# Softplus of a state-space layer: six of eight correction subtractions on GpSimd instead of VectorE, and "one plus the exponential" on VectorE in every round

## Chip, cores and metric

The kernel runs on one core of one Trainium2 chip. The metric is the device time of one execution in microseconds (us); the number given for a kernel is the median of several runs. Five engines matter: TensorE (PE in the profile's rows, PEld for its weight loads), VectorE (DVE), ScalarE (ACT), GpSimd (POOL) and SyncE (SP), which only issues transfers.

## What is computed

A small language-model tower on 8 x 256 tokens, 192 channels wide: embedding and position code, one Mamba layer that scans in both directions, and a mixture of eight experts. The part that the change touches is the step size `dt` of the scan, one array for each direction:

```python
proj = u @ x_proj_w
dt = jax.nn.softplus(proj[..., :DT_RANK] @ dt_w + dt_b)
...
y = selective_scan(u, dt, A, Bm, Cm)       # dA = exp(dt * A); h = dA * h + dt * u * B
```

`u` has 384 inner channels, kept as 3 blocks of 128 partitions.

## The kernel before

The tokens are cut into four groups of 512 (`NG = 4`, `GT = 512`), and each group has two directions, so the softplus stage has eight rounds, n = 0 to 7, with group n // 2 and direction n % 2. One round works on an array of 128 partitions x 1536 float32 (three blocks of 512 tokens). [...]

- TensorE: three products into PSUM (L1543). They wait on `s_pl`, which says that VectorE has read round n-2 out of the same banks.
- ScalarE: |x| block by block (L1232), e = exp(-|x|) (L1234, into `sp_e`, signalled by `s_e`), then log(1 + e) (L1240, into `dt`, signalled by `s_l`).
- w = 1 + e. In rounds 0, 2, 4, 6 and 7 VectorE computes it (L797); in rounds 1, 3 and 5 (`BY_ACT`) ScalarE does (L1242, signalled by `s_w`).
- The correction (w - 1) - e, which is what rounding lost in 1 + e: L798 on VectorE, signalled by `s_c`. This is the function `correction`.
- `add_pos` (L807): dt = max(x, 0) + log(1 + e), read from PSUM and `dt`, on VectorE, signalled by `s_pl`.
- `subtract_correction` (L814): dt = dt - correction, on VectorE, signalled by `s_dt`. In rounds 4 and 5 a product dt * u of rounds 0 and 1 follows (`times_u`, L817).

`sp_e` and `sp_w` have three buffers each (`SP = 3`), so ScalarE waits on `s_dt` of round n-3 before it begins round n.

The order on each engine is the order in which its program is written; the engines meet only at semaphores. GpSimd gathers the embedding rows first (L561), then helps with one mix of the embedding (L583, L586), adds the residual (L597), and has nothing in the softplus stage. It comes back in the scan, where it multiplies each scanned state by C (L625).

The scan follows (L851 on VectorE). Its first item waits for round 7 on VectorE (`s_dt` of 8), for ScalarE's decays exp(dt * A) (L1278, which wait for `s_dt` of 7) and for the products of TensorE (L1451 and L1573 in `x_blocks_of`). The first two `x_blocks_of` wait on `s_pl` of 7 and 8, since they write into banks that `add_pos` reads. ScalarE then evacuates transposes of dt * u (L1211), and goes on to the second unit of the scan (L1261, L1264, L1278).

Of the kernel before, what the change touches and what calls it, by code (L numbers as in the profile page):

```python
# [8 lines left out]
ALU = mybir.AluOpType  # L9
ACT = mybir.ActivationFunctionType  # L10
# [28 lines left out]
SP = 3  # L39
# [36 lines left out]
def build(nc, tok, emb, spos, pos, chan, w_in, gb_in, xproj, dt_w, gb_out, w_out, merge, w_route, emb_t,  # L76
          energy, fatigue, gates12, b1, b2, wf1, ws1, hf1, wf2, ws2, hf2, gates_dram, b_rows, x_rows, y_rows, out):
    ctx = ExitStack()
    with ctx:
# [3 lines left out]
        def sem(name):  # L83
            return ctx.enter_context(nc.semaphore(name))
# [62 lines left out]
        def cut(shape, dt=FP32, parts=P):  # L147
            n = 1
            for s in shape:
                n *= s  # L150
            words = n if dt != BF16 else n // 2
            assert used[0] + words <= ARENA, used[0]
            v = arena[0:parts, used[0]:used[0] + words]
            used[0] += words
            if dt != FP32:
                v = v.bitcast(dt)
            if len(shape) == 2:
                v = v.rearrange("p (a b) -> p a b", b=shape[1])
            if len(shape) == 3:
                v = v.rearrange("p (a b c) -> p a b c", b=shape[1], c=shape[2])  # L160
            if len(shape) == 4:
                v = v.rearrange("p (a b c d) -> p a b c d", b=shape[1], c=shape[2], d=shape[3])
            return v
# [6 lines left out]
        dt_all = [[cut([DB, GT]) for _ in range(2)] for _ in range(NG)]  # L170
# [47 lines left out]
        sp_e, sp_w = zip(*[[cut([DB, GT]) for _ in range(2)] for _ in range(SP)])  # L218
# [114 lines left out]
        s_e = sem("softplus_exp_ready")  # L333
        s_c = sem("softplus_corr_ready")
        s_pl = sem("softplus_pos_and_log_added")
        s_w = sem("softplus_one_plus_exp_ready")
        s_l = sem("softplus_log_ready")
        s_lb_ps = sem("dt_and_b_product")
        s_lb = sem("dt_and_b_rows_ready")
# [5 lines left out]
        s_dt = sem("dt_ready")  # L345
# [73 lines left out]
        s_passed = sem("waits_passed")  # L419
        FRONT_LOADS, PAR_LOADS = 2, 34  # L420
        DT_BANK = 2
        BY_ACT = (1, 3, 5)
        FIRST_BANKS = (0, 0, 0, 1, 0, 1, 0, 1)

        c_rows = b_rows
# [130 lines left out]
        def _(pool):  # L556
            g_ = nc.gpsimd
            st = Steps(pool, p_step)
# [35 lines left out]
            for h in range(2):  # L594
                half = slice(HT * h, HT * (h + 1))
                pool.wait_ge(s_lnin, h + 1)
                g_.tensor_tensor(resid[:, half, :], resid[:, half, :], ln_in[:, half, :], ALU.add).then_inc(s_res, 1)  # L597

            def times_u(g, d):

                pool.wait_ge(s_dtu_ps, TG * (2 * g + d))
                g_.tensor_tensor(dtu, dt_all[g][d], u_all[g], ALU.mult).then_inc(s_dtu, 1)
# [5 lines left out]
            for i in range(ITEMS):  # L608
# [7 lines left out]
                e, part = divmod(i - 3 * DB, EACH * DB)  # L616
# [42 lines left out]
        def _(dve):  # L659
            v = nc.vector  # L660
            st = Steps(dve, v_step)
# [128 lines left out]
            def correction(n):  # L790

                w, e = sp_w[n % SP], sp_e[n % SP]
                dve.wait_ge(s_e, n + 1)
                if n in BY_ACT:
                    dve.wait_ge(s_w, BY_ACT.index(n) + 1)
                else:
                    st.then(v.tensor_scalar(w, e, 1.0, None, ALU.add))  # L797
                v.scalar_tensor_tensor(w, w, -1.0, e, ALU.add, ALU.subtract).then_inc(s_c, 1)  # L798

            def add_pos(n):  # L800

                g, d = divmod(n, 2)
                dt = dt_all[g][d]
                dve.wait_ge(s_l, n + 1)
                bank = ps[:, DT_BANK + DB * d:DT_BANK + DB * (d + 1), :].rearrange("p a b -> p (a b)")
                flat = dt.rearrange("p a b -> p (a b)")
                v.scalar_tensor_tensor(flat, bank, 0.0, flat, ALU.max, ALU.add).then_inc(s_pl, 1)  # L807

            def subtract_correction(n):
                g, d = divmod(n, 2)  # L810
                dt = dt_all[g][d]
                dve.wait_ge(s_pl, n + 1)
                dve.wait_ge(s_c, n + 1)
                v.tensor_tensor(dt, dt, sp_w[n % SP], ALU.subtract).then_inc(s_dt, 1)  # L814

            def times_u(d):
                v.tensor_tensor(dtu_b if d else dtu, dt_all[0][d], u_all[0], ALU.mult).then_inc(s_dtu, 1)  # L817

            for n in range(2 * NG):
                if n in BY_ACT:  # L820
                    add_pos(n)
                    correction(n)
                else:
                    correction(n)
                if n == 0:
                    dve.wait_ge(s_rset, 1)
                    st.then(v.tensor_copy(gain_1[:], ps[:, 1, 0:E]))
                    v.tensor_copy(w_route_sb[:, :, E + DR + 1:RC], ps[0:KC, 1, E:(1 + KT) * E].rearrange("p (k e) -> p k e", k=KT)).then_inc(s_wr, 1)
                if n not in BY_ACT:
                    add_pos(n)  # L830
                subtract_correction(n)
                if n in (4, 5):
                    dve.wait_ge(s_dt, n - 3)
                    times_u(n - 4)
# [266 lines left out]
        def _(act):  # L1101
            a = nc.scalar
            a.preload_act_table_set("natural_log_exp_and_others")
            st = Steps(act, a_step)
# [61 lines left out]
            def keep_lb(g):  # L1166
                act.wait_ge(s_lb_ps, g + 1)
                if g >= 2:

                    act.wait_ge(s_c_st[g % 2], 32)  # L1170
                a.activation(lb[g % 2], ps[:, 0, :], ACT.Identity, scale=row_scale[:], bias=row_one[:]).then_inc(s_lb, 1)
# [36 lines left out]
            def keep_first_dtu_t(i):  # L1208

                act.wait_ge(s_dtu_ps, i + 1)  # L1210
                a.activation(dtu_t[0][i // TG][:, i % TG, :], ps[:, FIRST_BANKS[i], 0:DI], ACT.Copy).then_inc(s_dtu_t, 1)  # L1211

            def keep_bt(g):
                act.wait_ge(s_bt_ps, g + 1)
                a.activation(bt[:, TG * g:TG * (g + 1), :], ps[:, 1, 0:TG * 2 * NS].rearrange("p (t n) -> p t n", t=TG), ACT.Copy).then_inc(s_bt, 1)

            a.preload_act_table_set("natural_log_exp_and_others")
            for g in range(NG):
                for d in range(2):
                    n = 2 * g + d  # L1220
                    if n >= SP:

                        act.wait_ge(s_dt, n - SP + 1)

                    if n == 0:
                        act.wait_ge(s_u, NG * DB)
                    if n == 2:
                        act.wait_ge(s_sz_st, 16 * NG)
                    dt = dt_all[g][d]
                    for blk in range(DB):  # L1230
                        act.wait_ge(s_dt_ps, DB * n + blk + 1)
                        st(a.activation(dt[:, blk, :], ps[:, DT_BANK + DB * d + blk, :], ACT.Abs))  # L1232
                    st.wait()
                    a.activation(sp_e[n % SP], dt, ACT.Exp, scale=-1.0).then_inc(s_e, 1)  # L1234
                    if d == 1:
                        keep_bt(g)
                        if g == NG - 1:
                            keep_first_dtu_t(1)
                    act.wait_ge(s_e, n + 1)
                    a.activation(dt, sp_e[n % SP], ACT.Ln, bias=1.0).then_inc(s_l, 1)  # L1240
                    if n in BY_ACT:
                        a.activation(sp_w[n % SP], sp_e[n % SP], ACT.Identity, bias=1.0).then_inc(s_w, 1)  # L1242
                    if d == 0 and g + 1 < NG:
                        keep_lb(g + 1)
                    elif d == 0:
                        act.wait_ge(s_res, 2)
                        act.wait_ge(s_xn, NG)
                        act.wait_ge(s_xn_ps, NG)
                        keep_first_dtu_t(0)
# [196 lines left out]
        def _(pe):  # L1446
# [111 lines left out]
            def x_blocks_of(i):  # L1558

                u, blk = divmod(i, DB)  # L1560
                g, _, d = unit_of(u)
                cols = slice(P * blk, P * blk + P)
                if blk == 0:
                    pe.wait_ge(s_x_t, u + 1)
                    pe.wait_ge(s_dtu_t, 8 * g + TG * (d + 1))
                if i >= 2:

                    pe.wait_ge(s_scan, i - 1)
                bank = X_BANK + PAIR * (i % 2)
                for t in range(TG):  # L1570
                    transpose(ps[:, bank, P * t:P * t + P], x_t[u % 2][:, t, cols], P)
                for t in range(TG):
                    last = mm(ps[:, bank + 1, P * t:P * t + P], dtu_t[g % 2][d][:, t, cols], b_diag[u % 2][:, t, :], start=True, stop=True)  # L1573
                last.then_inc(s_x_ps, 1)
# [270 lines left out]
```

## Time and profile before

| | us |
|---|---|
| median of 3 runs (lowest, highest) | 904.82 (903.65, 904.99) |
| the profiled execution, device time | 903.25 |
| its span, first to last instruction | 901.5 |
| softplus stage on VectorE, first L797 to first scan L851 | 94.0 to 144.3 |
| busy in that stretch: VectorE, ScalarE, GpSimd | 49.35, 48.75, 0.00 |
| GpSimd from the end of L597 to its first L625 | 66.4 to 146.7 |

The page of the profile gives busy shares over the whole span. This change lies within one stretch of about 50 us, so the shares are to be read from that stretch. A row's duration runs from the start of an instruction on its engine to its end; where it waits inside for something that no semaphore shows, the wait is in the duration.

### The profile page before, as it was taken

To read this page: it belongs to the slowest core of one execution; us is meant where nothing else is said; L and a number is where in the kernel's file an instruction comes from. 1 tells how busy PE (TensorE), PEld (TensorE's weight loads), DVE (VectorE), ACT (ScalarE), POOL (GpSimd) and SP (SyncE) were. 2 spreads that over 40 slices of the span, in tenths; PEclk is the share of its full clock that TensorE was granted. 3 is DMA by queue.
4 is the path that set the end of the run, shared out by engine and by line. 5 is a ranking of instruction groups with operands and counts; after the bars stand their busy time and mean duration, and the time that the engine had idled before them with its cause. 6 is when DMAs were issued, how large, how long until landed. Compare 5 with 4: busy or idle time off the path is not lost.

```text
span 901.5 us, 16654 instructions
## 1 busy us (share of the span) xinstructions
PE 778.9 (86%) x6060; PEld 706.4 (78%) x6061; DVE 730.8 (81%) x871; ACT 648.5 (72%) x1261; POOL 535.1 (59%) x343
## 2 busy tenths in 40 slices
PE   0389777899999999989999899996956999999990
PEld 0133336899998999989999899995855899999990
DVE  3788899789999899988999999998938455555554
ACT  0365999999999999989999999992331444444421
POOL 6430004799988999969999799892000444444420
PEclk9999988999999999999999999997955899999996
DMA  4003103355674754745746466376450111111106
GB/s 87 3 30 111 9 27 123 89 137 175 148 212 149 165 191 123 195 140 130 210 113 163 159 180 187 118 167 230 136 171 9 40 44 44 44 44 44 44 23 218
DMA packets 46453, 104.43 MB, mean 116 GB/s; under 512 B 16448, under 2 KB 25176, under 8 KB 46392
## 3 DMA queue, kind: packets, MB, share of 16 engines
q1 hardware_dynamic: 35784, 74.67, 25.6%
q0 software_dynamic: 8352, 27.07, 15.1%
q10 hardware_dynamic: 2256, 1.87, 0.6%
q8 instruction: 38, 0.62, 0.3%
q14 instruction: 23, 0.19, 0.1%
HBM read 83.77 MB, written 19.82 MB: 115 GB/s over the span
## 4 chain that ended last, share of the span: by engine, by line
PE 47%; DVE 22%; ACT 17%; POOL 7%; issue 4%; DMA 2%; DVEq 0%; ACTq 0%; POOLq 0%; SPq 0%
PE ps L1451 15%; PE ps L1755 8%; PE ps L1573 8%; DVE arena L851 8%; ACT arena L1278 6%; PE ps L1738 6%; POOL arena L625 5%; ACT arena L1261 4%; PE ps L1743 4%; ACT arena L1264 3%; PE ps L1471 2%; PE ps L1474 1%; DVE stats L672 1%; DVE arena L798 1%; PE ps L1673 1%
## 5 line engine op out<-in xcount | busy, mean ns | idle before, releaser
L625 POOL TENSOR_TENSOR arena<-arena 128x1024 f32<-128x1024 f32 x192 | 395.3, 2285 | 117.3 <-DVE arena L851 114.0
L851 DVE TENSOR_TENSOR_SCAN arena<-arena,ps 128x1024 f32<-128x1024 f32 x192 | 426.3, 2277 | 20.1 <-PE ps L1573 16.9
L1451 PE MATMUL ps<-ident,arena 128*128 128x128 f32 (+3 forms) x2622 | 349.3, 280 | 79.2 <-ACT arena L1139 37.7
L1451 PEld LDWEIGHTS ps<-ident,arena 128*128 128x128 f32 (+3 forms) x2622 | 299.7, 144 | 100.6 <-issue 52.0
L1278 ACT ACTIVATE arena<-arena,neg_a 128x510 f32<-128x510 f32 x384 | 241.0, 708 | 0.1
L629 POOL DMA_INDIRECT arena<-x_rows,arena x39 | 37.8, 970 | 160.2 <-DVE arena L1035 79.6
L1573 PE MATMUL ps<-arena,ln_in 128*128 128x128 f32 x768 | 104.0, 279 | 0.0
L1573 PE MATMUL ps<-arena 128*128 128x128 f32 x768 | 101.4, 275 | 0.0
L1573 PEld LDWEIGHTS ps<-arena,ln_in 128*128 128x128 f32 x768 | 96.0, 196 | 0.0
L1573 PEld LDWEIGHTS ps<-arena 128*128 128x128 f32 x768 | 93.3, 192 | 0.0
L1755 PE MATMUL ps<-arena,ln_in 128*128 x468 | 82.7, 327 | 0.8 <-DVE arena L1066 0.8
L1264 ACT ACTIVATE arena<-ident,arena 128x128 f32<-128x128 f32 x256 | 81.0, 388 | 0.0
L1755 PEld LDWEIGHTS ps<-arena,ln_in 128*128 128x128 f32 x468 | 75.1, 190 | 1.2 <-issue 1.1
L1261 ACT ACTIVATE arena<-ln_in,arena 128x384 f32<-128x384 f32 x128 | 68.1, 605 | 3.1 <-PE ps L1573 2.7
L1261 ACT ACTIVATE arena<-arena 128x384 f32<-128x384 f32 x128 | 67.9, 602 | 2.6 <-PE ps L1573 2.5
L637 POOL DMA_INDIRECT y_rows<-arena x39 | 38.5, 988 | 30.9 <-DVE arena L1066 19.1
L1409 ACT ACTIVATE arena<-ps 128x256 f32<-128x256 f32 x39 | 15.0, 384 | 56.2 <-PE ps L1451 56.2
L1053 DVE TENSOR_TENSOR ln_in<-ps,arena 128x384 f32<-128x384 f32 x40 | 22.1, 554 | 40.1 <-PE ps L1743 40.1
L1053 DVE TENSOR_TENSOR ln_in<-ps,ln_in 128x384 f32<-128x384 f32 x38 | 21.0, 553 | 34.3 <-PE ps L1743 34.3
L1417 ACT ACTIVATE arena<-arena 128x1158 f32 x20 | 23.4, 1170 | 33.4 <-issue 14.2
L1061 DVE SCALAR_TENSOR_TENSOR ln_in<-ln_in 128x384 f32<-128x384 f32 x78 | 43.5, 558 | 2.7
L1417 ACT ACTIVATE ln_in<-arena 128x1158 f32 x19 | 22.2, 1170 | 20.9 <-issue 17.4
(218 smaller groups left out, 882.5 us busy)
## 6 DMA issues: line engine op xcount, KB each, us to landing
arena<-b_rows SPq DMA_DIRECT2D x64, 512.0 KB, 4.0
arena<-ws SPq DMA_DIRECT2D x16, 576.0 KB, 6.3
arena<-wf POOLq DMA_DIRECT2D x16, 576.0 KB, 8.2
arena<-hf POOLq DMA_DIRECT2D x16, 576.0 KB, 7.9
summed_first<-arena SPq DMA_DIRECT2D x8, 576.0 KB, 5.4
summed_second<-arena SPq DMA_DIRECT2D x8, 576.0 KB, 7.3
arena<-summed_second SPq DMA_DIRECT2D x8, 576.0 KB, 5.8
gates_dram<-arena SPq DMA_DIRECT2D x4, 768.0 KB, 3.4
```

Of the source, the lines that this page charges most:

```text
L625: g_.tensor_tensor(state[i % STATES], state[i % STATES], c_bc[u % C_BUFS], ALU.mult).then_inc(s_mul, 1)
L851: v.tensor_tensor_scan(o, a, x, 0.0, ALU.mult, ALU.add).then_inc(s_scan, 1)
L1053: added = v.tensor_tensor(hid, ps[:, H_BANKS[half] + i, 0:HH].rearrange("p (a b) -> p a b", b=P), bias[:, 3 * i:3 * (i + 1)].unsqueeze(2). ...
L1061: v.scalar_tensor_tensor(hid, hid, 0.0, hid, ALU.max, ALU.mult).then_inc(s_h[i], 1)
L1261: a.activation(x_t[u % 2][:, t, :], dtu_t[g % 2][d][:, t, :], ACT.Copy, scale=bt[:, TG * g + t, col:col + 1])
L1264: last = a.activation(b_diag[u % 2][:, t, :], ident[:], ACT.Copy, scale=bt[:, TG * g + t, col:col + 1])
L1278: last = a.activation(out_a[:, n, :, lo:hi], src[:, :, lo:hi], ACT.Exp, scale=neg_a[:, blk, d, PAIR * pair + n:PAIR * pair + n + 1])
L1417: a.activation(w1_cur[half], w1_all[:, bass.ds(e * WC, WC)], ACT.Copy).then_inc(s_wc, 1)
L1451: return mm(o, src, ident[at:at + parts, at:at + parts], start=start, stop=True, is_transpose=True, skip_group_check=True)
L1573: last = mm(ps[:, bank + 1, P * t:P * t + P], dtu_t[g % 2][d][:, t, cols], b_diag[u % 2][:, t, :], start=True, stop=True)
L1738: mm(ps[:, H_BANKS[half] + j // 3, P * (j % 3):P * (j % 3) + P], w1_cur[half][:, P * j:P * j + P], slot_x_t[half][:, 0, :], start=j % 3 == ...
L1755: last = mm(ps[:, 3, 0:C], h_t[half][:, j, :], w2_all[:, bass.ds(e * (HB * C) + j * C, C)], start=j == 0, stop=j == HB - 1)
```

## The change

Four edits. ScalarE no longer computes 1 + e in rounds 1, 3 and 5; VectorE does so in all eight rounds, and the order on VectorE is the same in all (1 + e, correction, add). In rounds 0 to 5 (`BY_POOL = 6`) the subtraction of the correction is issued on GpSimd, in order of n, each waiting for `s_pl` and `s_c` of its round; it is placed behind L597, ahead of the scan. In rounds 6 and 7 it stays on VectorE and waits for the earlier ones (`s_dt` of n).

```diff
-        BY_ACT = (1, 3, 5)
+        BY_POOL = 6
...
+            for n in range(BY_POOL):
+                dt = dt_all[n // 2][n % 2]
+                pool.wait_ge(s_pl, n + 1)
+                pool.wait_ge(s_c, n + 1)
+                g_.tensor_tensor(dt, dt, sp_w[n % SP], ALU.subtract).then_inc(s_dt, 1)
...
                 dve.wait_ge(s_e, n + 1)
-                if n in BY_ACT:
-                    dve.wait_ge(s_w, BY_ACT.index(n) + 1)
-                else:
-                    st.then(v.tensor_scalar(w, e, 1.0, None, ALU.add))
+                st.then(v.tensor_scalar(w, e, 1.0, None, ALU.add))
                 v.scalar_tensor_tensor(w, w, -1.0, e, ALU.add, ALU.subtract).then_inc(s_c, 1)
...
                 dve.wait_ge(s_pl, n + 1)
                 dve.wait_ge(s_c, n + 1)
+                dve.wait_ge(s_dt, n)
                 v.tensor_tensor(dt, dt, sp_w[n % SP], ALU.subtract).then_inc(s_dt, 1)
...
             for n in range(2 * NG):
-                if n in BY_ACT:
-                    add_pos(n)
-                    correction(n)
-                else:
-                    correction(n)
+                correction(n)
...
-                if n not in BY_ACT:
-                    add_pos(n)
-                subtract_correction(n)
+                add_pos(n)
+                if n >= BY_POOL:
+                    subtract_correction(n)
                 if n in (4, 5):
                     dve.wait_ge(s_dt, n - 3)
                     times_u(n - 4)
...
                     a.activation(dt, sp_e[n % SP], ACT.Ln, bias=1.0).then_inc(s_l, 1)
-                    if n in BY_ACT:
-                        a.activation(sp_w[n % SP], sp_e[n % SP], ACT.Identity, bias=1.0).then_inc(s_w, 1)
```

VectorE's program before, from the first softplus instruction through round 1 (`arena` is the buffer that holds dt, e and w, `ps` is PSUM; the names in brackets are the semaphores waited for):

```order
L797 TENSOR_SCALAR arena<-arena 128x1536 [waits softplus_exp_ready]
L798 SCALAR_TENSOR_TENSOR arena<-arena 128x1536 [waits vector_step]
L827 COPY gain<-ps 128x8 [waits router_setup_product]
L828 COPY w_route_sb<-ps 96x2x8 [waits vector_step]
L807 SCALAR_TENSOR_TENSOR arena<-ps,arena 128x1536 [waits softplus_log_ready]
L814 TENSOR_TENSOR arena<-arena 128x1536 [waits softplus_corr_ready,softplus_pos_and_log_added]
L807 SCALAR_TENSOR_TENSOR arena<-ps,arena 128x1536 [waits softplus_log_ready]
L798 SCALAR_TENSOR_TENSOR arena<-arena 128x1536 [waits softplus_one_plus_exp_ready,softplus_exp_ready]
L814 TENSOR_TENSOR arena<-arena 128x1536 [waits softplus_corr_ready,softplus_pos_and_log_added]
```

The same place after the change (line numbers shift: L799 is 1 + e, L800 the correction, L809 the addition):

```order
L799 TENSOR_SCALAR arena<-arena 128x1536 [waits softplus_exp_ready]
L800 SCALAR_TENSOR_TENSOR arena<-arena 128x1536 [waits vector_step]
L826 COPY gain<-ps 128x8 [waits router_setup_product]
L827 COPY w_route_sb<-ps 96x2x8 [waits vector_step]
L809 SCALAR_TENSOR_TENSOR arena<-ps,arena 128x1536 [waits softplus_log_ready]
L799 TENSOR_SCALAR arena<-arena 128x1536 [waits softplus_exp_ready]
L800 SCALAR_TENSOR_TENSOR arena<-arena 128x1536 [waits vector_step]
L809 SCALAR_TENSOR_TENSOR arena<-ps,arena 128x1536 [waits softplus_log_ready]
```

The subtraction L814 is gone from both rounds, and right behind each addition that reads PSUM now stands the 1 + e of the next round; in round 1 the addition has moved behind the correction.

GpSimd's program after the change, from the residual addition to the first multiplications of the scan (L596 is what was L597, L630 what was L625):

```order
L596 TENSOR_TENSOR resid<-resid,ln_in 128x1536 [waits ln_in_ready,conv_ready,params_loaded]
L596 TENSOR_TENSOR resid<-resid,ln_in 128x1536 [waits ln_in_ready]
L602 TENSOR_TENSOR arena<-arena 128x1536 [waits softplus_corr_ready,softplus_pos_and_log_added] x6
L630 TENSOR_TENSOR arena<-arena 128x1024 [waits scan_done,c_broadcast_loaded_0]
L630 TENSOR_TENSOR arena<-arena 128x1024 [waits scan_done] x2
```

The six subtractions (L602 there) are new in this place; before the change the multiplications of the scan came next.

## Rows read from the trace of the kernel before

**Rows 1.** The page, busy time of each engine over the span.

```profile
PE 778.9 (86%) x6060; PEld 706.4 (78%) x6061; DVE 730.8 (81%) x871; ACT 648.5 (72%) x1261; POOL 535.1 (59%) x343
```

**Rows 2.** Busy time of each engine in the softplus stage.

```profile
core 0: us, PE busy (x) PEld busy (x) DVE busy (x) ACT busy (x) POOL busy (x), PEclk, DMA share, GB/s
94.00:144.30 50.30, 37.51 (x110) 19.58 (x110) 49.35 (x34) 48.75 (x69) 0.00 (x0) 0.83 0.05 15
```

**Rows 3.** Chain that ended last: start, length in us, engine and line.

```profile
104.24 1.76 DVE arena L814
106.00 0.88 DVE arena L797
106.91 1.76 DVE arena L798
108.67 1.68 DVE arena L807
...
136.35 1.15 DVE arena L814
...
145.19 0.88 ACT ln_in L1211 x2
```

**Rows 4.** Groups of instructions in the softplus stage: busy us, mean ns | idle before.

```profile
L814 DVE TENSOR_TENSOR arena<-arena 128x1536 f32<-128x1536 f32 x8 | 14.1, 1759 | 0.5
L798 DVE SCALAR_TENSOR_TENSOR arena<-arena 128x1536 f32<-128x1536 f32 x8 | 14.0, 1754 | 0.2
L807 DVE SCALAR_TENSOR_TENSOR arena<-ps,arena 128x1536 f32<-128x1536 f32 x8 | 14.0, 1751 | 0.2 <-ACT arena L1240 0.2
...
L797 DVE TENSOR_SCALAR arena<-arena 128x1536 f32<-128x1536 f32 x5 | 4.8, 955 | 6.4 <-ACT arena L1234 6.4
...
L1242 ACT ACTIVATE arena<-arena 128x1536 f32<-128x1536 f32 x3 | 4.4, 1472 | 0.0
```

**Rows 5.** Timeline of VectorE, first addition, later subtractions, end of stage: start, us.

```profile
96.97 1.75 DVE L807 SCALAR_TENSOR_TENSOR arena<-ps,arena 128x1536 f32<-128x1536 f32 x1
...
136.35 1.76 DVE L814 TENSOR_TENSOR arena<-arena 128x1536 f32<-128x1536 f32 x1
...
140.69 1.75 DVE L807 SCALAR_TENSOR_TENSOR arena<-ps,arena 128x1536 f32<-128x1536 f32 x1
142.47 1.76 DVE L814 TENSOR_TENSOR arena<-arena 128x1536 f32<-128x1536 f32 x1
144.27 6.64 DVE L851 TENSOR_TENSOR_SCAN arena<-arena,ps 128x1024 f32<-128x1024 f32 x3
```

**Rows 6.** Timeline of VectorE in the embedding, while GpSimd computes too.

```profile
37.81 0.69 DVE L706 TENSOR_TENSOR ln_in<-arena 128x512 f32<-128x512 f32 x1
38.53 1.43 DVE L706 TENSOR_TENSOR arena<-arena 128x512 f32<-128x512 f32 x1
40.00 1.43 DVE L709 TENSOR_TENSOR ln_in<-ln_in,arena 128x512 f32<-128x512 f32 x1
```

**Rows 7.** Timeline of GpSimd in the same stretch.

```profile
37.86 1.56 POOL L583 TENSOR_TENSOR ln_in<-arena 128x512 f32<-128x512 f32 x1 [11.46 <-DVE arena L696]
39.50 1.39 POOL L583 TENSOR_TENSOR arena<-arena 128x512 f32<-128x512 f32 x1
```

**Rows 8.** GpSimd arithmetic of single lines (ns min/median/max), and two of its timeline.

```profile
L602 POOL TENSOR_TENSOR arena<-arena x6: 2907/3226/3564, 178.5 to 451.1; 128x1536 f32<-128x1536 f32 x6
L597 POOL TENSOR_TENSOR resid<-resid,ln_in x2: 3445/3446/3447, 59.5 to 62.9; 128x1536 f32<-128x1536 f32 x2
...
174.61 4.62 POOL L625 TENSOR_TENSOR arena<-arena 128x1024 f32<-128x1024 f32 x2
178.53 3.56 POOL L602 TENSOR_TENSOR arena<-arena 128x1536 f32<-128x1536 f32 x1
```

**Rows 9.** Timeline of ScalarE: exponential of round 1, and the evacuation behind round 7.

```profile
97.66 1.49 ACT L1234 ACTIVATE arena<-arena 128x1536 f32<-128x1536 f32 x1
...
145.19 0.87 ACT L1211 ACTIVATE ln_in<-ps 128x384 f32<-128x384 f32 x2 [0.66 <-PE ps L1451]
```

More of the change, by code:

```diff
@@ L335, in build @@
         s_pl = sem("softplus_pos_and_log_added")
-        s_w = sem("softplus_one_plus_exp_ready")
         s_l = sem("softplus_log_ready")
```

## Prediction

> **What bounds the kernel now.** I read the page first: TensorE is busy 86% of the span, VectorE 81%, ScalarE 72%, GpSimd 59% [rows 1]. None of these says what the change is worth, because it lies within one stretch. So the second view is the busy time between the first L797 and the first scan. There VectorE works 49.35 of 50.3 us, ScalarE 48.75, GpSimd nothing [rows 2]. Third, the chain that ended last: from the addition of round 1 on it runs through VectorE alone (subtract, 1 + e, correction, add, and again), until the subtraction of round 6 at 136.35 hands over to ScalarE and TensorE, which lead to ScalarE's evacuation at 145.19 [rows 3]. VectorE is the bound of the stage, and ScalarE, at 97% of it, is close behind. Whatever happens to VectorE's pace here shifts the whole rest of the kernel; a gain is capped early by ScalarE, a loss is capped by nothing.
>
> **What the edits do on paper.** Durations run start to start, since back-to-back operations on VectorE overlap by some 0.08 us: the chain has L797 from 106.00 to 106.91, and L798 to L807 takes 1.76, L807 to the next 1.68-1.70 [rows 3]. I use 0.95 for 1 + e, 1.70 for the others.
>
> - Six subtractions leave VectorE: 6 x 1.70 = 10.2 us less.
> - Three 1 + e come to VectorE: 3 x 0.95 = 2.9 us more.
> - Three L1242 leave ScalarE: 4.4 us less [rows 4].
> - GpSimd gets six subtractions of 128x1536. Nearest rows: its products of the same shape in the same buffer, 2.907 us at the least, and the residual addition, 3.446 us [rows 8]. The longer ones of L602 are counted from a start that lies inside the operation before: 178.53 is ahead of 174.61 + 4.62 = 179.23, where L625 ends, so that one ran 178.53 + 3.56 - 179.23 = 2.86 us. I take 2.9, because L602 reads and writes the same buffer as the new operation; L597 is the upper end.
>
> If the two engines did not disturb each other, VectorE would have 7.3 us less, ScalarE 4.4 us less, and the stage would gain about 5.
>
> **What they do to each other.** In the embedding both engines work on two-input operations with all operands in SBUF, and they take turns. VectorE's 128x512 operation takes 0.69 us when it is first [rows 6]. The next one starts at 38.53, takes 1.43 and ends at 39.96, while GpSimd's operation of 37.86 ends at 39.42 [rows 6, 7]: it finished 0.54 us behind GpSimd's end, so it stood still until then. GpSimd's next starts at 39.50 and ends at 40.89, which is 0.93 behind VectorE's end at 39.96; VectorE's next starts at 40.00 and ends at 41.43, 0.54 behind 40.89. So one runs while the other stands, for the whole length of an operation, and the one already waiting goes first: GpSimd had asked at 39.50, before VectorE's third operation at 40.00, and was served before it.
>
> In the changed stage the correction (L798) has two SBUF inputs, like those. The addition (L807) reads PSUM and one SBUF input. The scan has that form as well (L851, arena and ps in [rows 5]) and the products of GpSimd under it take their 2.9 us, so I let it run beside GpSimd. For 1 + e (L797) no row shows it beside GpSimd. It has one input, but takes 955 ns where the two-input form takes 1759 for the same 1536 elements [rows 4], so it moves one input at nearly twice the pace, as with both read paths; I take it as excluded too. Below that stands the case that it runs freely (priced under the rivals).
>
> The Trainium skill ("SBUF — State Buffer", section "Who interferes with whom") states that a `tensor_scalar` in a two-port mode takes the port pair that VectorE and GpSimd share, and that the second to issue blocks fully. By that rule the total is the one forecast here; with the exclusion for two-input operations alone it would be that of the third rival. The trace has no row that decides it.
>
> **The sum.** The subtraction of round n may start when the addition of round n has ended. At that moment VectorE goes on with 1 + e of round n+1, and GpSimd asks some 0.1 us later. Whichever gets in first, the correction of round n+1 is behind both: 0.95 + 2.9 + 1.7, and only then comes the addition, 1.7. A round takes 7.2 us, less 0.1 to 0.15 that an operation saves when it was already issued and waited (0.54 against 0.69 above), so 7.1, where it was 0.95 + 3 x 1.7 = 6.05 in the rounds with 1 + e on VectorE and 5.1 to 5.2 in the others. GpSimd's work is on VectorE's path in full. Nothing of it hides under the addition, because the addition of the same round is what it waits for, and the one of the next round is behind a correction that GpSimd has shut out.
>
> Step by step, from the addition of round 0, which ends at 96.97 + 1.75 = 98.72 as before [rows 5]:
>
> - Round 1: e is ready at 97.66 + 1.49 = 99.15 [rows 9], GpSimd holds until 101.75, 1 + e until 102.55, correction 104.25, addition 105.9.
> - Rounds 2, 3, 4: 7.1 each: 113.0, 120.1, 127.2.
> - Round 5: dt * u of round 0 is ahead (1.7): 136.0.
> - Round 6: dt * u of round 1 (1.7), GpSimd (2.85), 1 + e (0.8), correction, addition: 144.8; the subtraction on VectorE ends at 146.5. Its new wait for `s_dt` of 6 costs nothing: GpSimd finished round 5 at 140.5.
> - Round 7: no more GpSimd, 0.95 + 1.7 + 1.8 + 1.75 = 6.2: 152.7, against 142.47 + 1.76 = 144.23 [rows 5].
>
> That is 8.5 us later. The same as a sum: six times 2.9 on (17.4), 10.2 off, 2.9 on, 0.9 off for the six starts that were already issued, and 0.7 off for the small gaps before L814 and L807 (0.5 and 0.2 idle) [rows 4], which go.
>
> **Who waits for that.** ScalarE kept up with rounds of 5.6 us on average, so it keeps up with 7.1, and the 4.4 us it saves are worth nothing. The addition of round 7 ends at 150.9 instead of 140.69 + 1.75 = 142.44, and behind it stand TensorE's second `x_blocks_of` and the transposes that ScalarE takes at 145.19, after waiting 0.66 us for them [rows 9]; that was on the chain, and it moves by the same 8.5. ScalarE's decays wait for the subtraction of round 6, which moves from 136.35 + 1.76 = 138.1 to 146.5 [rows 5], and take less than 4 us, so they are done before the transposes come. On SyncE the loads of C and of the weights behind `s_dt` of 8 shift along. Against the profiled execution, 903.25 + 8.5 = 911.8; the median of the runs lies 1.6 higher, 904.8, so the forecast for a median is 913.3.
>
> With 3.45 for GpSimd's operation it is 6 x 0.55 = 3.3 more, 916.6. The Trainium skill ("GPSIMD Engine Reference", section "Elementwise — side-by-side cycle accounting") has 4497 ns for a two-input add of 2048 elements; as an estimate from that page 1536 take 3.37, and the total would be 916.1. The row of L602 is shorter, that of L597 a little longer than it.
>
> **Rivals.**
>
> 1. *No disturbance that matters* (8%), ending on the other side. The stage gains what ScalarE allows, between its 4.4 us and VectorE's 7.3; about 5, so 899.8. For it: GpSimd is empty here, and in the scan the two engines run together freely. Against: rows 6 and 7. It would decide if the correction, a three-operand form, used the read paths otherwise than L706 does; a round would have to be below 5.6 us.
> 2. *VectorE keeps its turn* (7%): the correction gets in ahead of the waiting GpSimd. Then GpSimd's 2.9 lies over the addition, a round is 0.95 + 1.7 + 2.9 = 5.6, about the average of before, and the total is 904 to 906. Against: the order of service at 39.96.
> 3. *1 + e runs beside GpSimd* (10%): six times 0.8 to 0.95 are hidden, about 5.4: 907.9.
> 4. *The forecast's mechanism with GpSimd near 3.45 us* (13%): 916.6.
>
> The forecast itself has 60%, other outcomes 2%. That leaves slower by over 0.2% (above 906.6; about what this measurement can tell from no change) at 0.86, within 0.2% at 0.05, faster at 0.09. The range runs from 906.5, which takes in rival 3, to 918, which takes in rival 4 with a little for slower handovers.
>
> **What would show it.** The profile after should have GpSimd's six subtractions end about 2.9 us behind the end of VectorE's 1 + e; corrections in rounds 1 to 5 of about 4.5 us instead of 1.75 (or, if GpSimd is served first, 1 + e of about 3.8); additions unchanged at 1.75 and 7.1 us apart; the first scan near 152.7; no idle time of VectorE before 1 + e put down to ScalarE beyond 1 us. Wrong it would be if corrections stay at 1.75 (rival 1), if GpSimd's operations are stretched to 4.6 while rounds stay at 5.6 (rival 2), or if ScalarE or TensorE turn out to be waited for in these rounds.

## The result, and the profile after

The changed kernel takes 914.62 us (median of 4 runs, 914.13 to 915.65), the kernel before 904.24 (4 runs, 903.40 to 904.99): a ratio of 1.0117, with a 95% interval of 1.0099 to 1.0134. On paper the change takes 7 us of work off the engine that bounds the stage, and the kernel gets 10.4 us slower. A second measurement, on another chip (r_after below, 5 runs against 17 of the kernel before), gives 8.5 us and 1.0100, so the size is known to about 2 us only. One of the five runs of a further experiment, d_warm, took 1384 us at a mean granted clock of 0.565; its ratio leaves that run out.

The profiled execution after took 915.65 us, the longest of its four. Its softplus stage begins 1.6 us later than before (first 1 + e at 95.61 instead of 94.02); that lies ahead of everything that was changed, and the last section comes back to it. So times in the stage are compared from its first 1 + e.

The timeline of VectorE after the change (start, length in us, line and operation; L799 is 1 + e, L800 the correction, L809 the addition, L820 dt * u, L850 the scan):

```profile
98.56 1.74 DVE L809 SCALAR_TENSOR_TENSOR arena<-ps,arena 128x1536 f32<-128x1536 f32 x1
100.77 3.34 DVE L799 TENSOR_SCALAR arena<-arena 128x1536 f32<-128x1536 f32 x1 [0.46 <-ACT arena L1233]
104.14 1.76 DVE L800 SCALAR_TENSOR_TENSOR arena<-arena 128x1536 f32<-128x1536 f32 x1
105.82 1.75 DVE L809 SCALAR_TENSOR_TENSOR arena<-ps,arena 128x1536 f32<-128x1536 f32 x1
107.49 0.95 DVE L799 TENSOR_SCALAR arena<-arena 128x1536 f32<-128x1536 f32 x1
108.47 4.34 DVE L800 SCALAR_TENSOR_TENSOR arena<-arena 128x1536 f32<-128x1536 f32 x1
112.74 1.74 DVE L809 SCALAR_TENSOR_TENSOR arena<-ps,arena 128x1536 f32<-128x1536 f32 x1
...
121.98 3.21 DVE L799 TENSOR_SCALAR arena<-arena 128x1536 f32<-128x1536 f32 x1 [0.59 <-ACT arena L1233]
...
128.57 1.75 DVE L820 TENSOR_TENSOR arena<-arena 128x1536 f32<-128x1536 f32 x1
130.24 3.67 DVE L799 TENSOR_SCALAR arena<-arena 128x1536 f32<-128x1536 f32 x1
...
154.34 2.29 DVE L850 TENSOR_TENSOR_SCAN arena<-arena,ps 128x1024 f32<-128x1024 f32 x1 [0.35 <-PE ps L1570]
```

And that of GpSimd, the first two and the fifth of its six subtractions:

```profile
100.39 2.91 POOL L602 TENSOR_TENSOR arena<-arena 128x1536 f32<-128x1536 f32 x1 [32.81 <-DVE arena L809]
107.65 3.55 POOL L602 TENSOR_TENSOR arena<-arena 128x1536 f32<-128x1536 f32 x1 [4.36 <-DVE arena L809]
...
128.74 4.35 POOL L602 TENSOR_TENSOR arena<-arena 128x1536 f32<-128x1536 f32 x1 [4.36 <-DVE arena L809]
```

Read the two together. GpSimd's first subtraction runs from 100.39 to 103.30, undisturbed, in 2.91 us. VectorE's 1 + e was started at 100.77, in the middle of it, and ends at 104.11: 0.81 after GpSimd's end. In the next round VectorE was first: its 1 + e of 107.49 takes its usual 0.95, GpSimd asks at 107.65 and ends at 111.20, which is 2.76 after the end of 1 + e at 108.44. The correction started at 108.47, so behind GpSimd in the queue, and ends at 112.81, 1.61 after GpSimd. The additions, which read PSUM, keep their 1.75. In [rows 4] the same 1 + e took 955 ns on average and the correction 1754.

The chain that ended last, from the products of round 7 to the evacuation of the last transposes:

```profile
137.42 5.50 PE ps L1540 x6
142.92 0.02 issue
142.94 0.61 ACT arena L1231
143.55 0.02 issue
143.57 1.49 ACT arena L1233
...
145.60 1.38 ACT arena L1239
...
151.41 1.09 PE ps L1448 x4
...
157.27 0.88 ACT ln_in L1210 x2
```

Before the change VectorE led until 137.5, and only the last 7.7 us up to this point were ScalarE and TensorE [rows 3]. Now the last 20 us are. The waits in the stage (engine and line, what it waited for, us, times, longest) say why:

```profile
ACT arena L1231 <- PE ps L1540: 14.4, 13, 2.6
PE ps L1540 <- DVE arena L809: 14.2, 5, 3.8
```

TensorE waits 14.2 us for VectorE's additions to free the banks, where it was 7.3 before, and ScalarE waits 14.4 us for TensorE. The last evacuation comes 157.27 - 95.61 = 61.66 us after the first 1 + e, against 145.19 - 94.02 = 51.17: 10.5 later, where the first scan is 58.73 - 50.25 = 8.5 later. In the second profiled execution of the changed kernel (r_after) it is 10.0 and 8.2.

### The profile page after: what moved, and what is told of

Same layout as the page of the kernel before. It is cut to its first block, busy times and chain, and to the rows that moved or that the text cites. A ratio compares the mean times of both kernels' runs of the same rounds, so it can differ in the third digit from the quotient of the medians.

```text
span 913.9 us, 16651 instructions
## 1 busy us (share of the span) xinstructions
PE 782.8 (86%) x6060; PEld 705.7 (77%) x6061; DVE 738.7 (81%) x868; ACT 645.1 (71%) x1258; POOL 556.4 (61%) x349
## 4 chain that ended last, share of the span: by engine, by line
PE 47%; DVE 20%; ACT 20%; POOL 6%; issue 4%; DMA 2%; DVEq 0%; ACTq 0%; POOLq 0%; SPq 0%
PE ps L1448 14%; PE ps L1752 8%; ACT arena L1275 7%; DVE arena L850 7%; PE ps L1570 7%; PE ps L1735 6%; ACT arena L1258 5%; POOL arena L630 4%; PE ps L1740 4%; ACT arena L1261 3%; PE ps L1468 2%; PE ps L1540 1%; PE ps L1471 1%; ACT arena L1283 1%; DVE stats L677 1%
## 5 line engine op out<-in xcount | busy, mean ns | idle before, releaser
L850 DVE TENSOR_TENSOR_SCAN arena<-arena,ps 128x1024 f32<-128x1024 f32 x192 | 426.5, 2276 | 21.8 <-PE ps L1570 16.9
L630 POOL TENSOR_TENSOR arena<-arena 128x1024 f32<-128x1024 f32 x192 | 395.1, 2285 | 54.1 <-DVE arena L850 50.8
L602 POOL TENSOR_TENSOR arena<-arena 128x1536 f32<-128x1536 f32 x6 | 21.6, 3602 | 52.6 <-DVE arena L809 52.6
```

The lines of the kernel that those rows point to most:

```text
L630: g_.tensor_tensor(state[i % STATES], state[i % STATES], c_bc[u % C_BUFS], ALU.mult).then_inc(s_mul, 1)
L850: v.tensor_tensor_scan(o, a, x, 0.0, ALU.mult, ALU.add).then_inc(s_scan, 1)
```

## The experiments

Theory: VectorE and GpSimd take turns, whenever VectorE's operation has two inputs in SBUF or is the 1 + e, and GpSimd reads from SBUF; the loss is GpSimd's reading, laid across VectorE's line. Rivals: the loss comes from dt being ready later; from three VectorE operations in every round; from TensorE and ScalarE feeding the stage.

All runs in one table. "Scan" is the start of the first scan, "evacuation" the start of ScalarE's last evacuation of transposes behind round 7, both from the profiled execution and in us after the first 1 + e. The ratio is to runs of the kernel before on the same chip.

| kernel | scan | evacuation | median us | ratio (95%) |
|---|---|---|---|---|
| before | 50.25 | 51.17 | 904.24 | |
| changed | 58.73 | 61.66 | 914.62 | 1.0117 (1.0099-1.0134) |
| r_after, the same again | 58.40 | 61.19 | 913.79 | 1.0100 (1.0085-1.0114) |
| a_ones_only | 53.07 | 55.36 | 907.2 | 1.0025 (1.0015-1.0036) |
| b_pool_only | 52.37 | 52.70 | 906.51 | 1.0013 (1.0003-1.0022) |
| c_pool_late | 50.64 | 52.59 | 905.52 | 1.0000 (0.9991-1.0009) |
| d_warm | 58.08 | 59.48 | 914.31 | 1.0103 (1.0085-1.0121) |
| r_warm, the same again | 58.06 | 59.79 | 914.46 | 1.0107 (1.0092-1.0123) |
| e_junk_read | 65.52 | 67.24 | 919.82 | 1.0165 (1.0143-1.0188) |
| f_junk_write | 50.26 | 51.61 | 904.53 | 0.9994 (0.9984-1.0004) |
| g_late_act | 48.80 | 49.30 | 903.35 | 0.9984 (0.9976-0.9993) |
| r_late_act, the same again | 48.80 | 49.31 | 903.59 | 0.9978 (0.9969-0.9987) |
| h_late_warm | 50.67 | 51.56 | 904.79 | 0.9996 (0.9985-1.0007) |
| i_late_act3 | 50.22 | 51.44 | 904.39 | 0.9998 (0.9988-1.0008) |

### One half of the change at a time

a_ones_only: 1 + e on VectorE in all rounds, nothing on GpSimd.

```diff
-        BY_POOL = 6
+        BY_POOL = 0
```

> One plus the exponential on VectorE in all eight rounds, all eight subtractions on VectorE, nothing on GpSimd. Taking turns (my theory): without GpSimd nothing is stretched, every 1 + e stays at 0.95 us and every correction at 1.76; VectorE has three more 1 + e (2.9 us) and loses some 0.9 of small gaps, so the first scan is about 2 us later and the time about 906.3. Rival (the loss comes from the chain of three operations in every round and from ScalarE and TensorE feeding it, not from GpSimd): most of the 10 us is here, above 911.

Measured: 1.0025, first scan 2.8 us later (2 were expected; fewer of the small gaps went than the 0.9 us counted, and the scan waits 0.36 us for TensorE), 1 + e and correction at 0.95 and 1.76 throughout. It is a quarter of the loss at most in the time; the rival with most of 10 us here falls.

b_pool_only: the kernel before, with the six subtractions on GpSimd.

```diff
+            for n in range(6):
+                dt = dt_all[n // 2][n % 2]
+                pool.wait_ge(s_pl, n + 1)
+                pool.wait_ge(s_c, n + 1)
+                g_.tensor_tensor(dt, dt, sp_w[n % SP], ALU.subtract).then_inc(s_dt, 1)
...
+                dve.wait_ge(s_dt, n)
...
-                subtract_correction(n)
+                if n >= 6:
+                    subtract_correction(n)
```

> Only the subtractions of rounds 0 to 5 go to GpSimd; ScalarE keeps 1 + e of rounds 1, 3 and 5, and the order in those rounds is add, then correct. Taking turns: in the odd rounds GpSimd's operation lies over the addition that reads PSUM, and in the even ones over nothing, so a pair of rounds takes 0.95 + 2.9 + 1.7 + 1.7 + 2.9 + 1.7 = 11.85 us where it took 11.2; three pairs give about 2 us, time about 906. Rival (GpSimd's operation costs its full length in every round, six times 2.9 less 1.7): 7 us later, 911.

Measured: 1.0013, first scan 2.1 us later, both as expected. The way there was not the expected one. Two of VectorE's rows (L813 is the addition, L803 is 1 + e), and GpSimd's fourth subtraction:

```profile
101.42 1.76 DVE L813 SCALAR_TENSOR_TENSOR arena<-ps,arena 128x1536 f32<-128x1536 f32 x1 [2.00 <-ACT arena L1248]
...
119.96 0.96 DVE L803 TENSOR_SCALAR arena<-arena 128x1536 f32<-128x1536 f32 x1 [3.19 <-ACT arena L1242]
```

```profile
116.91 2.90 POOL L603 TENSOR_TENSOR arena<-arena 128x1536 f32<-128x1536 f32 x1 [1.76 <-DVE arena L804]
```

VectorE waits 7.3 us for ScalarE within this stage, where it was 0.2 before, and GpSimd's first and fourth subtractions lie mostly over such waits. So the expected 2 us came out in part by luck. The same six operations on GpSimd cost 2 us here, and 8.5 - 2.8 = 5.7 on top of a_ones_only in the changed kernel. That shows that the length of GpSimd's operation alone does not set the price. How much of it the additions from PSUM hide, and how much the waits for ScalarE, this run does not separate; the next one moves the operations onto the additions by themselves.

### The same operations, started at another moment

c_pool_late: one number of the changed kernel.

```diff
-                pool.wait_ge(s_c, n + 1)
+                pool.wait_ge(s_c, n + 2)
```

> The changed kernel, but GpSimd's subtraction of round n also waits for the correction of round n+1, so that it starts beside the addition of round n+1, which reads PSUM. Taking turns: a round takes 0.95 + 1.7 + 2.9 = 5.55 us instead of 7.1, corrections stay at 1.76, the 1 + e of the next round is stretched to about 2; the first scan comes about 1 us earlier than in the kernel before, time 903 to 905. Rival (what costs is how long GpSimd takes, or that dt comes late): starting it later can only make it later, 914 or more.

Measured: 1.0000, first scan at 50.64. VectorE's rounds, from its timeline:

```profile
108.44 1.75 DVE L809 SCALAR_TENSOR_TENSOR arena<-ps,arena 128x1536 f32<-128x1536 f32 x1
110.11 2.28 DVE L799 TENSOR_SCALAR arena<-arena 128x1536 f32<-128x1536 f32 x1
112.42 1.76 DVE L800 SCALAR_TENSOR_TENSOR arena<-arena 128x1536 f32<-128x1536 f32 x1
114.10 1.75 DVE L809 SCALAR_TENSOR_TENSOR arena<-ps,arena 128x1536 f32<-128x1536 f32 x1
```

and GpSimd's:

```profile
108.67 2.91 POOL L602 TENSOR_TENSOR arena<-arena 128x1536 f32<-128x1536 f32 x1 [2.75 <-DVE arena L800]
114.33 2.90 POOL L602 TENSOR_TENSOR arena<-arena 128x1536 f32<-128x1536 f32 x1 [2.75 <-DVE arena L800]
```

GpSimd starts with the addition, overlaps all of it, and stretches the next 1 + e by 1.3 us only; additions are 114.10 - 108.44 = 5.66 apart instead of 6.9 to 7.3. GpSimd's operation starts one correction later than in the changed kernel, every dt is ready later against its own round, and the kernel is 9 us faster. That settles between turn-taking and lateness as the cause of the loss. The first scan was expected 1 us earlier than in the kernel before, and comes 0.4 later, since the subtraction of round 6 waits for GpSimd, which the expectation had not counted:

```profile
137.67 1.76 DVE L817 TENSOR_TENSOR arena<-arena 128x1536 f32<-128x1536 f32 x1 [1.51 <-POOL arena L602]
```

Lateness does have a smaller price: ScalarE, which reuses the buffers, waits 0.48 us for GpSimd ahead of round 6 and 1.73 us ahead of round 7, and the evacuation comes 1.4 us later than in the kernel before.

### Reading or being busy

Both add six GpSimd operations to the kernel before, that nothing in the stage waits for; what they write is not used. (SyncE's later weight loads into the same memory also wait for them, but the sixth product ends at 145.42, and those loads wait for the last subtraction, which starts at 159.19.)

```diff
+            for n in range(6):
+                pool.wait_ge(s_pl, n + 1)
+                if n:
+                    pool.wait_ge(s_junk, n)
+                g_.tensor_tensor(scratch, scratch, ones[:].unsqueeze(1).to_broadcast([P, 12, P]), ALU.mult).then_inc(s_junk, 1)
```

In f_junk_write the last line is `g_.memset(scratch, 1.0)`.

> The kernel before, unchanged in what it computes, and beside it six GpSimd products of 128x1536 on memory that nobody uses, each started when the addition of rounds 0 to 5 has ended; nothing waits for them in the stage. Taking turns: 6 x 3.0 = 18 us of reading by GpSimd lie across VectorE's line, less the two additions of rounds 1 and 3 (3.4) and the starts already issued (0.9): the first scan comes about 13.5 us later, time about 918, with VectorE's two-input operations of 4.3 us among them. Rival (the loss comes from dt being ready late, that is from the dependency): nothing, 905.

> The same with a fill of 128x1536 by GpSimd, which reads nothing, in place of the product. If the turns are about reading from SBUF, VectorE's corrections and subtractions keep their 1.76 us, and at most a 1 + e is stretched: below 906.5. If any activity of GpSimd stops VectorE, corrections or subtractions are stretched by the length of the fill.

Measured: e_junk_read 1.0165, first scan 65.52 - 50.25 = 15.3 us later; f_junk_write 0.9994. VectorE in e_junk_read, first around GpSimd's second product, then around its fifth (L823 is the subtraction, L826 dt * u):

```profile
103.85 3.06 DVE L807 SCALAR_TENSOR_TENSOR arena<-arena 128x1536 f32<-128x1536 f32 x1
107.01 4.81 DVE L823 TENSOR_TENSOR arena<-arena 128x1536 f32<-128x1536 f32 x1
...
132.14 1.76 DVE L823 TENSOR_TENSOR arena<-arena 128x1536 f32<-128x1536 f32 x1
133.81 4.98 DVE L826 TENSOR_TENSOR arena<-arena 128x1536 f32<-128x1536 f32 x1
```

GpSimd's fifth product in the same run:

```profile
132.18 5.00 POOL L606 TENSOR_TENSOR arena<-arena,ones 128x1536 f32<-128x1536 f32 x1 [6.04 <-DVE arena L816]
```

It asked 0.04 us after VectorE's subtraction had begun, stood until 133.90, and ran 3.28 us; VectorE's next, started at 133.81, ends 1.61 after it. That is 0.3 us longer than the 3.0 I had used, six times, which is the difference between the 13.5 expected and the 15.3 measured. Nothing depends on these products, so the dependency plays no part.

f_junk_write, GpSimd's first two fills:

```profile
100.41 1.39 POOL L606 MEMSET arena<- 128x1536 f32 x1 [32.77 <-DVE arena L816]
104.17 1.38 POOL L606 MEMSET arena<- 128x1536 f32 x1 [2.38 <-DVE arena L816]
```

and VectorE's subtraction and correction over them:

```profile
100.38 1.76 DVE L823 TENSOR_TENSOR arena<-arena 128x1536 f32<-128x1536 f32 x1
...
104.03 1.75 DVE L807 SCALAR_TENSOR_TENSOR arena<-arena 128x1536 f32<-128x1536 f32 x1
```

Neither is stretched by anything, and the same holds for the other four fills. A GpSimd that is busy with writing alone does not hold VectorE's two-input operations; one that reads does. (A fill is also shorter than the product and does no arithmetic; that difference is not tested apart from the reading.) In this run no 1 + e met a fill, so for that pair it says nothing.

### TensorE's clock

d_warm and r_warm: useless transposes keep TensorE busy ahead of three rounds of the changed kernel.

```diff
+                    if 2 * g + d in (4, 6, 7):
+                        if d:
+                            pe.wait_ge(s_bt, g)
+                        for _ in range(30):
+                            transpose(ps[:, d, 0:P], ident[:], P)
```

> The changed kernel with 30 transposes of the identity, whose results nobody reads, on TensorE ahead of the products of rounds 4, 6 and 7, where it had been idle for 3.5 to 3.8 us and its three products then took 5.17, 4.51 and 5.49 us instead of 2.8. If TensorE's granted clock behind the idle time is what makes the evacuation behind round 7 come 10.5 us later and not 8.5: the products of round 7 take about 2.8 us, round 4 loses its idle 0.6 us on VectorE, and the time is 912 to 913. If it is ScalarE's own work that is late: no change, 914.6.

> The changed kernel once more, on the same chip as the three below, so that each can be set against it. All theories: about 1.2% above the kernel before.

> The kernel with the 30 transposes ahead of rounds 4, 6 and 7 again, beside the changed kernel. TensorE's clock accounts for the 2 us between the first scan (8.5 us later) and the evacuation (10.5): 1.5 to 2 us below the changed kernel. ScalarE's own work accounts for it: equal.

Busy time in one stretch around the products of round 4 (columns: stretch, its length, then busy us and count of PE, PEld, DVE, ACT, POOL, then granted clock), changed kernel:

```profile
110.00:122.00 12.00, 8.20 (x18) 3.65 (x17) 11.37 (x6) 7.16 (x10) 5.28 (x3) 0.72 0.00 0
```

and d_warm:

```profile
110.00:122.00 12.00, 10.22 (x49) 6.26 (x49) 11.93 (x7) 9.08 (x10) 5.28 (x3) 1.00 0.01 1
```

In the changed kernel the mean granted clock of these 12 us is 0.72, a mixture of full speed (2.4 GHz) and half (1.2 GHz), after 3.8 us of idling; with the useless work it is 1.00, and the products of round 4 take 2.84 us instead of 5.17. But the kernel before is not at full speed either, which the expectations left out: in the same 12 us its granted clock is 0.86, its products of round 4 take 4.29 us, and those of round 7:

```profile
126.84 4.54 PE L1543 MATMUL ps<-arena 128*128 128x512 f32 x6 [1.12 <-DVE arena L807]
```

The 0.59 us that VectorE stood idle ahead of round 4 are gone, but r_after, without useless work, does not have them either (its products of round 4 took 4.51 us). The evacuation comes 2.2 us earlier in d_warm than in the changed kernel, and 1.4 us earlier in r_warm than in r_after. In d_warm the products of round 7 still took 4.54 us, against the 2.8 expected. In r_warm they took 2.84, and then TensorE had to wait for VectorE's addition of round 7 (L810 there) before the last products:

```profile
150.68 1.12 PE L1449 MATMUL ps<-ident,arena 128*128 128x128 f32 x4 [1.78 <-DVE arena L810]
```

The time does not follow: 914.46 against 913.79 on the same chip, where 1.5 to 2 us less were expected. In the profiled execution of r_warm 1.8 us come back later, in the scan (last section). So the profiles show that TensorE's clock moves the evacuation by 1.4 to 2.2 us, but that filling the idle time gains anything was not shown, and whether the loss in the scan is chance or a consequence stays open.

> The late version with 30 transposes of the identity on TensorE ahead of the products of rounds 6 and 7. In the late version the evacuation behind round 7 comes 1.4 us later against the start of the stage than in the kernel before, the first scan only 0.4. If the clock of TensorE is the difference: 1 us below the late version.

The same on the late version: evacuation at 51.56 instead of 52.59, as expected, and a time of 0.9996 against 1.0000 (each to the kernel before on its own chip), which the intervals do not tell apart. The 1 us less in the time was not found.

### A version that beats both

g_late_act: c_pool_late, and ScalarE computes 1 + e of rounds 3 and 5, ahead of its logarithm.

```diff
+        BY_ACT = (3, 5)
...
+                if n in BY_ACT:
+                    dve.wait_ge(s_w, BY_ACT.index(n) + 1)
+                else:
+                    st.then(v.tensor_scalar(w, e, 1.0, None, ALU.add))
...
+                    if n in BY_ACT:
+                        a.activation(sp_w[n % SP], sp_e[n % SP], ACT.Identity, bias=1.0).then_inc(s_w, 1)
```

> The late version (GpSimd's subtraction of round n behind the correction of round n+1), with 1 + e of rounds 3 and 5 on ScalarE, ahead of the logarithm. It takes 2 x 0.95 us off the line that VectorE and GpSimd share, and ScalarE, which waits for TensorE there, has room for 2 x 1.4. Expected: 1 to 1.9 us below the late version, about 0.1 to 0.2% below the kernel before. If ScalarE has no room: equal or above.

> The version with rounds 3 and 5 on ScalarE once more, for its size: 0.1 to 0.2% below the kernel before, if the first result holds; within 0.1% if it was chance.

Measured: 0.9984 and 0.9978, both clear of 1, which is 0.2% or about 1.8 us. The first scan comes 1.84 us earlier than in the late version, 0.85 of it in round 3 and 0.98 in round 5, and 1.45 earlier than in the kernel before. ScalarE's room is used up in round 3: ahead of the correction VectorE waits for its 1 + e (L1245):

```profile
111.57 1.76 DVE L805 SCALAR_TENSOR_TENSOR arena<-arena 128x1536 f32<-128x1536 f32 x1 [1.38 <-ACT arena L1245]
```

i_late_act3 does it in round 1 as well:

> The late version with 1 + e of rounds 1, 3 and 5 on ScalarE, ahead of the logarithm. In the version with rounds 3 and 5 VectorE already stood idle for 1.38 us ahead of round 3 and 0.85 ahead of round 4, waiting for ScalarE. If ScalarE is the bound there: the third one gains nothing, 0 to 1 us above the version with two, first scan at 48.8 us from the start of the stage or later. If VectorE and GpSimd still are: 0.9 us earlier.

Measured: first scan at 50.22, 1.4 us later than with two. Its VectorE waits for ScalarE:

```profile
101.12 1.76 DVE L805 SCALAR_TENSOR_TENSOR arena<-arena 128x1536 f32<-128x1536 f32 x1 [2.07 <-ACT arena L1245]
...
117.05 0.96 DVE L804 TENSOR_SCALAR arena<-arena 128x1536 f32<-128x1536 f32 x1 [1.45 <-ACT arena L1238]
```

ScalarE is the bound by then. Of the placements tried here the best is 1.5 us ahead of the kernel before at the first scan.

## Why the prediction was right, and where it was off

**VectorE as the bound, and the turns.** Right, with its numbers. The ends of the additions, from the first 1 + e, were forecast at 11.9 (round 1), 19.0, 26.1, 33.2, 42.0 and 50.8 us, and the first scan at 58.7. Measured: 12.0, 18.9, 25.8, 33.0, 41.8, 50.5 and 58.73. The balance from the profile: the six stretched operations are 2.4, 2.6, 2.6, 2.3, 2.7 and 2.7 us longer than alone, 15.2 in all; idle time of 0.46 and 0.59; three 1 + e more, 2.9; six subtractions fewer, 10.1; small gaps gone, 1.0; and 0.3 more of waiting for TensorE ahead of the scan. That gives 8.4 us. The closeness of 8.5 is in part luck. For the six turns with the wait of round 1 the forecast had 17.4 - 0.9 = 16.5 us, and they took 15.2 + 0.46 = 15.7; the waits of 0.59 us in round 4 and 0.3 ahead of the scan, which it did not have, make up for that. In r_after the 0.59 is absent, and the scan comes 8.2 later. These waits (0.46 and 0.59 for ScalarE, 0.35 for TensorE) are also what the forecast had named as a sign against itself; the first stood in its own list, and together they are 1.4 of 58.7 us.

**1 + e excluded too.** This was the point that no row decided, with a rival at 907.9. It is decided by the first row of 1 + e above: 3.34 us instead of 0.95, started inside GpSimd's operation and ended behind it. The Trainium skill ("SBUF — State Buffer", section "Who interferes with whom") has both rules: a `tensor_scalar` in a two-port mode contends with GpSimd, and a two-input operation does so with a GpSimd operation that reads. The trace and f_junk_write (for the two-input form) agree.

**Who is served first.** Right: the operation that already waits goes ahead of one issued later. GpSimd's fifth subtraction had asked at 128.74, VectorE's 1 + e was started at 130.24, and GpSimd ran first. It was the rival "VectorE keeps its turn" that needed the opposite, and no round shows it. Which engine is first when both come free together varies: in rounds 1 and 4 GpSimd ran ahead of 1 + e since ScalarE had not delivered e, in rounds 2 and 3 the 1 + e was ahead. The sum is the same, as forecast.

**GpSimd's operation.** 2.9 us was taken, 2.91 alone and 2.76 after a wait was measured. The estimate from the Trainium skill's "GPSIMD Engine Reference" (section "Elementwise — side-by-side cycle accounting"), 3.37, is not borne out by this operation. The e_junk_read product took 3.28, so the operation, its layout or the form of its operands matters by 0.4 us; that was not taken further.

**Who waits for that.** Here a path was missed. The prediction hung the evacuation at 145.19 on the addition of round 7, so that it "moves by the same 8.5", and had ScalarE done long before. It moved by 10.5, and by 10.0 in r_after. In the profile ScalarE is not ready, because the products of round 7 come late. They wait for the addition of round 5, and start 137.42 - 95.61 = 41.8 us after the first 1 + e instead of 126.84 - 94.02 = 32.8. That is 9.0 later and not 8.5, since in round 5 the addition stood ahead of the correction in the kernel before and stands behind it now; the prediction's own list has this addition at 136.0, 9.2 later than before, but did not ask who waits for it. They then take 5.49 us instead of 4.54 (0.95), and from their end to the evacuation it is 14.4 us instead of 13.8 (0.55). Together that is 10.5.

TensorE idles for 3.5 to 3.8 us ahead of rounds 4, 6 and 7, and the mean granted clock from 136 to 146 is 0.66; in the kernel before it was 0.73 from 126 to 136, so TensorE was not at full speed there either. Of the 2.0 us by which the evacuation moves more than the first scan, 0.5 are the later start of these products, and 1.5 the slower work behind it. The wait that the prediction named is there as well: in r_warm, where the products of round 7 take 2.84 us, TensorE waits 1.78 us for the addition of round 7, and the evacuation is 59.79 - 51.17 = 8.6 later. The sentence that ScalarE "keeps up with 7.1" was wrong by 0.6 us in round 4 of one profile, and held in the other.

For the time of the kernel this stays undecided. The forecast of 913.3 was short by 1.3; the two measurements give 10.4 us (9.0 to 12.1) and 8.5 us (7.7 to 10.3), so that the first speaks for a shift of 10.5 and the second for one of 8.5, and the 1.4 to 2.2 us that d_warm and r_warm gained at the evacuation did not show in the time.

**No disturbance that matters**, the rival on the other side, falls with a_ones_only and c_pool_late: the kernel before plus 2.8 us of work is 0.25% slower, and the changed kernel is back at 1.0000 with one wait moved.

## What to carry to other kernels

An engine that is idle in a stage is not free capacity if it takes turns with the one that bounds the stage: ask, for each operation of both, where its inputs lie, and look for a stretch in which the two already ran together; the lengths there (0.69 against 1.43 us) gave this forecast to 0.2 us a round. If work of GpSimd that reads SBUF is moved beside VectorE all the same, start it beside an operation of VectorE that reads PSUM; one wait was worth 9 us here. And when an operation moves, list every engine that waits for it, not only the one at the end of the stage: here the missed path was from the addition of round 5 to the products of round 7.

## What the runs showed that was not expected

The profiled executions differ by steps of about 1.6 us in stretches that the kernels have in common. At one boundary between groups of the scan TensorE idles in the same way in both kernels, 1.04 and 2.0 us. The stretch right after it, in the kernel before:

```profile
392.00:396.00 4.00, 3.83 (x23) 3.83 (x24) 4.00 (x3) 2.72 (x6) 3.63 (x2) 0.67 0.14 41
```

and the same place in the changed kernel, 12 us later:

```profile
404.00:408.00 4.00, 3.74 (x34) 3.68 (x34) 4.00 (x3) 2.96 (x7) 3.54 (x2) 1.00 0.16 55
```

A granted clock of 0.67 against 1.00, 23 matmuls against 34, and VectorE then waits 1.20 us for TensorE in the one and not in the other. The interval between two neighbouring weight loads by GpSimd around it (L605 of the kernel before) is 60.4 us in the one and 58.7 in the other. Every profile has three such intervals, each of about 58.7 or 60.4 us; the changed kernel has its long one at the third. From the last evacuation to the end the twelve profiled kernels of the experiments take either 756.1 to 756.6 us or 758.1 to 758.4; in the first group one of the three intervals is long, in the second two are. The stage's start, at 94.0 in the kernel before and 95.6 in the changed one, differs by as much. Of that 1.2 us arise early: two neighbouring groups of TensorE's products, the first of which begins at 38.92 in both kernels, take 3.38 and 1.13 us in the one, 3.78 and 1.93 in the other. Why the clock falls after the same pause in one execution and not in another was not found. Whoever compares two profiles of this kernel for a difference of 2 us should compare stretches, not spans.
